# GpSimd splits a weight piece ahead of the normalisation, and issues the next piece's transfer between root and normalisation

## The reference

```python
q, k, v = x @ wq.T, x @ wk.T, x @ wv.T               # 16 heads of 8
attn = softmax(q @ k.T / sqrt(8) + slope[h] * -|i - j|)
x = layernorm(x + (attn @ v) @ wo.T + bo)
h = silu(x @ w1.T * s1) * (x @ w2.T * s2)
h = gelu(h @ h1.T * sh1)
h = gelu(h @ h2.T * sh2)
x = layernorm(x + h @ w3.T * s3)
```

## Time and profile before

| | us |
|---|---|
| median of 3 runs | 802.08 (801.79 to 804.29) |
| the profiled execution, its own time | 799.74 |
| its span, first to last instruction | 797.9 |
| outside the span | 1.84 |
| TensorE busy | 769.2 (96%) |
| VectorE busy | 630.1 (79%) |
| ScalarE busy | 611.7 (77%) |
| GpSimd busy | 313.4 (39%) |

### The profile page before, as it was taken

The page is one execution under the profiler, slowest core; times in us unless marked ns, Lnnn a source line. Parts: engine busy times, 40 slices in busy tenths (PEclk is TensorE's granted clock), DMA queues, the critical chain, the costliest instruction groups (busy, mean ns, idle before and its releaser), DMA issues.

```text
span 797.9 us, 26869 instructions
## 1 busy us (share of the span) xinstructions
PE 769.2 (96%) x10370; PEld 557.4 (70%) x10370; DVE 630.1 (79%) x1303; ACT 611.7 (77%) x1096; POOL 313.4 (39%) x490
## 2 busy tenths in 40 slices
PE   4999999999999999999999999999999999999995
PEld 2566666666666666666665788888888888888873
DVE  4789899899989999989993767777777776666774
ACT  5588787888888888878878777777777777777762
POOL 5346878787756657575634200000000000000001
PEclk9999999999999999999999999999999999999998
DMA  6755565656556565564621100111111111101001
GB/s 181 190 145 166 168 185 159 195 151 182 164 159 166 141 181 136 170 174 144 174 65 44 41 27 28 39 41 39 39 39 39 31 34 39 39 26 40 16 26 54
DMA packets 107341, 81.37 MB, mean 102 GB/s; under 512 B 11168, under 2 KB 94112, under 8 KB 107232
## 3 DMA queue, kind: packets, MB, share of 16 engines
q1 hardware_dynamic: 105632, 76.59, 34.1%
q0 software_dynamic: 880, 2.88, 1.3%
q10 hardware_dynamic: 720, 0.36, 0.2%
HBM read 45.72 MB, written 33.55 MB: 99 GB/s over the span
## 4 chain that ended last, share of the span: by engine, by line
PE 92%; DVE 2%; DMA 2%; issue 2%; ACT 1%; POOL 1%; SPq 0%; POOLq 0%; ACTq 0%; DVEq 0%
PE ps_b L951 17%; PE ps_b L954 17%; PE ps_o L523 15%; PE ps_a L464 11%; PE ps_b L472 6%; PE ps_b L579 4%; PE ps_a L951 3%; PE ps_a L954 3%; PE ps_a L548 2%; PE ps_a L479 2%; PE ps_b L540 2%; PE ps_a L562 2%; PE ps_b L479 2%; PE ps_b L570 1%; PE ps_b L534 1%
## 5 line engine op out<-in xcount | busy, mean ns | idle before, releaser
L762 DVE TENSOR_REDUCE neg_sb<-ps_a 128x2 f32<-128x512 f32 x512 | 324.7, 681 | 37.1 <-PE ps_a L479 29.7
L654 ACT ACTIVATE probs<-ps_b 128x512 f32<-128x512 f32 x512 | 281.4, 591 | 57.2 <-PE ps_b L479 57.1
L464 PE MATMUL ps_a<-qk_stack 52*64 52x256 bf16 x2048 | 178.0, 281 | 5.6 <-DMA qk_stack<-qk_scratch 2.8
L472 PE MATMUL ps_b<-qk_stack 54*64 54x256 bf16 x2048 | 172.3, 276 | 1.1 <-ACT probs L654 0.9
L1062 ACT ACTIVATE gelu_f<-ps_b,sc 128x512 f32<-128x512 f32 x124 | 85.5, 690 | 74.0 <-PE ps_b L954 66.4
L464 PEld LDWEIGHTS ps_a<-qk_stack 52*64 52x64 bf16 x2048 | 82.5, 108 | 79.4 <-DVE neg_sb L762 61.0
L523 PE MATMUL ps_o<-probs,v_aug 128*32 128x256 f32 x2048 | 137.3, 385 | 0.0
L1224 POOL TENSOR_SCALAR vareps_f<-meanvar_f 128x4 f32<-128x4 f32 x15 | 9.7, 644 | 301.0 <-DVE meanvar_f L1125 301.0
L479 PE MATMUL ps_a<-corner_sb,eye_sb 64*64 64x128 bf16 x1024 | 116.4, 222 | 0.3 <-issue 0.3
L479 PE MATMUL ps_b<-corner_sb,eye_sb 64*64 64x128 bf16 x1024 | 114.4, 218 | 0.0
L951 PE MATMUL ps_b<-g2h,h_hi 128*128 128x512 f32 x256 | 102.7, 401 | 0.0
(11 more groups left out here) (124 smaller groups left out, 1429.3 us busy)
## 6 DMA issues: line engine op xcount, KB each, us to landing
qk_stack<-qk_scratch SPq DMA_DIRECT2D x128, 192.0 KB, 3.4
qk_scratch<-qk_sb SPq DMA_DIRECT2D x64, 192.0 KB, 3.0
qk_scratch<-qk_sb SPq DMA_DIRECT2D x96, 128.0 KB, 3.0
xT_sb<-in_xT SPq DMA_DIRECT2D x32, 128.0 KB, 3.5
x_sb<-in_x SPq DMA_DIRECT2D x32, 128.0 KB, 3.4
x_scratch<-x_sb SPq DMA_DIRECT2D x32, 128.0 KB, 3.4
x_in<-x_scratch SPq DMA_DIRECT2D x32, 128.0 KB, 2.1
x_res<-x_scratch SPq DMA_DIRECT2D x32, 128.0 KB, 2.1
```

Of the source, the lines that this page charges most:

```text
L464: pe.matmul(ps[side * TILE:(side + 1) * TILE, qb * SEQ:(qb + 1) * SEQ], q_stack[i][rows_of, j, at:at + TILE], k_stack[i][rows_of, j, :], s ...
L472: pe.matmul(ps[side * TILE:(side + 1) * TILE, kb * SEQ:(kb + 1) * SEQ], k_stack[i][rows_of, j, at:at + TILE], q_stack[i][rows_of, j, :], s ...
L654: nc.scalar.activation(probs[:, h % HALF, :], ps_b[b_bank(t, k)][:], ACT.Exp, scale=slope[h]).then_inc(exp_done, 1)
L762: nc.vector.tensor_reduce(negmax[:, h_a // HALF, h_a % GROUPS, h_a % HALF // GROUPS, :], ps_a[a_bank(t, k)][:].rearrange("p (b k) -> p b k ...
```

## The change

In a step t the piece's two split instructions now stand ahead of `norm_x1`, and the transfer of the next piece stands inside it, behind the power instruction and ahead of the two normalising ones. Where a step has no `norm_x1` (step 1), the transfer stands at the step's end. No instruction is added or removed, and on the other engines and on SyncE's queue the order is as it was.

```diff
-def norm_x1(nc, pool, b, par, carried):
+def norm_x1(nc, pool, b, par, carried, meanwhile=None):
...
     nc.gpsimd.tensor_tensor(rstd[:], vareps[:], carried.minus_half[:, 0:BLK], ALU.pow).then_inc(carried.rstd_done, 1)
+    if meanwhile is not None:
+        meanwhile()
     wait(pool, carried.rstd_done, b + 1)
...
                 par = s % 2
-                if t + 1 in piece_at:
-                    load_piece(t + 1 - PIECE_FIRST)
                 if live(t, BATCH):
                     split_max(t, 1)
...
-                if live(t - 2, BATCH - 1):
-                    norm_x1(nc, pool, t - 2, par, carried)
                 if t in piece_at:
                     split_piece(t - PIECE_FIRST)
+                load = (lambda: load_piece(t + 1 - PIECE_FIRST)) if t + 1 in piece_at else None
+                if live(t - 2, BATCH - 1):
+                    norm_x1(nc, pool, t - 2, par, carried, load)
+                elif load is not None:
+                    load()
```

## The result

The change makes the kernel faster: 797.39 us median (796.43 to 799.16) against 801.46 us for the kernel before, over 8 runs each. The ratio is 0.9954 with a 95% interval of 0.994 to 0.9967, a gain of 2.6 to 4.8 us, or 4.07 us between the medians.

A forecast was written before the change was run, and what follows sets the result against it. TensorE was taken as the bound, with GpSimd costing time only through late heads 0 in piece steps. Their 1.36 us, taken as 1.4 off the median 802.08, gave 800.7 us, range 798.0 to 803.4.

The forecast's parts named there:

- What bounds the kernel, and the chain: TensorE bounds; GpSimd work between statistics and `split_max(t, 1)` pushes SyncE's queue, the rows of half 0 and head 0.
- late head: A step's head 0 with a ScalarE pause over 0.46 us, its maxima's rows issued late; five piece steps had one.
- The head start of 2.0 us: From L213 to `split_max(t, 1)`: comes 1.91 to 2.05 us sooner, taken as 2.0; 1.3 us in step 11.
- The sum: The five late heads' delays, 1.36 us, taken as 1.4 off the median: 802.08 - 1.4 = 800.7 us.
- 1.36 us off the profiled execution: Excess of five ScalarE pauses ahead of head 0 over 0.46 us, all gained: 799.74 to 798.4.
- the most that the change can be after: Loss of the piece steps' stretch against undisturbed steps of 12.64 us: 3.87 us, the gain's upper end.
- The 11 intervals: From L213 of step 2 to that of step 13, all piece steps: 142.91 us, predicted to become about 141.5.
- stops ahead of L579: TensorE waits in the piece steps, 1.30 us with no releaser and 0.8 twice; not tied to GpSimd-released transfers.
- No effect: Rival, chance 0.16: late heads come from SyncE's own varying issue times, its queue absorbs the head start; 802.1 us.
- All of the loss goes: Rival, chance 0.14: stops without a releaser are echoes of the crowding, so the whole 3.87 us go; 798.2 us.
- Slower by a transfer in a worse place: Rival, chance 0.12: the moved 256 KB starve TensorE's own instructions, adding 1.30 us stops; three would give 804.6 us.
- The paragraph on the transfer itself: The piece must land within 7.1 us of issue; slowest landing 4.2 us, so hidden with 2.9 us to spare.

The follow-up runs named there:

- the kernel with the shifted list: The kernel before with 128 more satisfied waits at the start of TensorE's list, the work the same: 809.38 us, ratio 1.0101.
- the kernel with three copies: The changed kernel plus three copies of a constant tile on GpSimd behind the normalisation in steps 2 to 12: 805.14 us, ratio 1.0038.

## Why the prediction was wrong in size

**What bounds the kernel, and the chain: right.** Statistics, GpSimd, `split_max(t, 1)`, SyncE's queue, rows of half 0, head 0. Two links were moved by themselves: GpSimd's stretch by moving the split and by added copies, the queue by its order. In the kernel before, a late head stands 2.74 to 2.77 us behind its rows' issue; in the other kernels, where no piece collides, mostly 2.74 to 2.82.

**The head start of 2.0 us: right.** 5.25 us became 3.26; in step 11, where 1.3 us was predicted, 4.59 became 3.47. The predicted 1.3 us or more of idle time ahead of L213 came out as 1.35 to 2.06. The issue cost what its row gave: L814 to L221 is 119.60 - 118.90 = 0.70 us. The Trainium skill, "DMA: Bandwidth & Descriptors", section "Latency and other measured facts", gives about 1 us to the first byte of a transfer that GpSimd issues. In the packet records of the kernel before, a piece's first packet begins 1.28 to 1.59 us after the start of the issue, which is more than the page has, and the measurement decides. What delays GpSimd's list is another quantity, the 0.65 us of the issue itself. The split in its new place takes 0.60 and 1.28 us, where it took 0.61 and 1.27. VectorE ran maxima out of PSUM beside it (L764, 126.86 to 129.34), so this agrees with the Trainium skill, "SBUF — State Buffer", section "Who interferes with whom", by which a VectorE operation contends there only if it has two inputs in SBUF or runs in a mode with two ports.

**The sum: the term that failed.** "1.36 us off the profiled execution" took the late heads of one execution for those of all. It was mis-sized: a second profile of the same kernel has 3.22, so the mean of the two is 2.3, and the kernel with the shifted list, whose GpSimd and SyncE lists are those of before, has 3.6. The change took all of it, since not one head 0 was late in either profile after. The upper end, "the most that the change can be after", failed by the same step: 3.87 us was the loss of one execution, and the second has 143.60 - 11 x 12.64 = 4.56. Two signs were there. Five delays between 0.08 and 0.63 us, each from a queue with no slack, are draws from something that varies, and slow issues were named as a rival and not as a reason for a larger mean. And the profiled execution ran 2.34 us under the median from which its loss was taken off; a typical execution may well lose more, though two profiles (1.36 us in one of 799.74, 3.22 in one of 800.77) can't show it.

**The rest.** The 11 intervals, as means of two profiles, went from (142.91 + 143.60)/2 = 143.26 to (140.05 + 140.94)/2 = 140.50, that is 2.76 us less. Of this 2.3 are the late heads; 0.5 are shorter stops ahead of L579 and L562, less than those stops vary between two profiles of one kernel (1.3 to 2.5 us before, 1.0 to 1.9 after), so from these four profiles alone they may be chance.

The other profiles speak for more. What the 11 intervals lose beside late heads is 1.3 to 3.5 us, in the mean 2.4, in six profiles with several late heads, and 0 to 1.9, in the mean 0.8, in seven with one or none (the kernel with three copies is left aside, since GpSimd's list bound it). So late heads, or the crowding behind them, seem to lengthen these stops too, by an amount that no experiment took by itself.

Outside the intervals the spans differ by another 0.6 us, half of it in the plain steps and half ahead of step 2, which no experiment settles. Together the spans went from a mean of 798.45 us (797.9 and 799.0) to 795.1 (794.6 and 795.6), 3.35 less, inside the interval of the runs. The base moved too: over 8 runs the kernel before had 801.46, and the forecast was set on 802.08.

**The rivals.** No effect: wrong. All of the loss goes: right in size (3.87 against 4.07), in part by luck. The stops ahead of L579 are not gone, with up to 1.03 us after, and the size fits because the late heads cost more than the rows showed; that the stops are in part echoes of the crowding is not refuted, as said above. Slower by a transfer in a worse place: it was given to TensorE's instructions; what the moved transfer delays is the small transfer of the maxima, and that would have decided had the split stayed where it was (1.0025). The paragraph on the transfer itself asked only whether the piece lands in time, not whose packets it meets; that it harmed nobody was right only in company with the split.

## What to carry to other kernels

Where an engine waits for the last item of a queue that issues without a pause, look at the slack of that item and not at the waits of one execution: without slack, slow issues ahead of it show up as lateness, another amount in each run, and one profile gives a poor mean. Such a loss can be removed at any link, and two removals don't add up: here moving GpSimd's split and reordering SyncE's queue each took all of it. Before a large transfer is moved, look which small, urgent one is issued at about the same moment: here a large one issued from 0.25 us ahead to 0.56 us behind did harm, and one issued 2 us behind did not.

## What the runs showed that had not been expected

A transfer of 256 KB issued from GpSimd's queue between 0.25 us ahead and 0.56 us behind two 4 KB transfers on SyncE's queue delayed what waited for the small ones by 1.1 to 1.6 us (3.82 to 4.31 us from issue to head 0, against 2.75), and one of 64 KB by 0.3 to 0.6. Issued 0.66 to 0.82 us behind, in three steps of three kernels, a 256 KB piece left 2.74 to 2.79 us; at 0.55 us one step shows no delay either, so the border is not sharp. The Trainium skill, "DMA: Bandwidth & Descriptors", section "Issuing engines are not separate DMA queues", says that transfers of different issuing engines run on the same DMA engines and interleave; the packet records agree: the last of the rows' packets ends at 84.57, among the piece's of 83.22 to 84.58.

An issue on SyncE's queue that mostly takes 0.5 us took up to 1.97 us (L358 at 105.91); why was not found. And 128 satisfied waits on TensorE put the next work off by 7.1 us against the first profile; since step 2 begins at 66.8 to 68.4 us in the other profiles, that is about 45 to 57 ns each (an estimate).
